# Attention in units of 256 tokens and four heads, with queries and keys from split float32r products

## The chip, the cores and the metric

The kernel runs on one core of a Trainium2 chip. The core has five engines with an instruction queue each: TensorE (PE, matmuls into PSUM), VectorE (DVE), ScalarE (ACT), GpSimd (POOL) and SyncE (SP, which here issues transfers). They run side by side and wait for each other by semaphores only. The metric is the device time of one launch in microseconds, lower is better.

## The reference

A model of four parts runs over 2,048 tokens of 128 channels: windowed attention, an FFN, a delta-rule layer with an MLP, and a routed FFN, with a layer norm behind each. Only the first part matters here:

```python
H, D, window_size = (16, 64, 32)
xn = x * rsqrt(mean(x * x) + 1e-6)
q, k, v = split(xn @ w_qkv.T, 3)              # each 2048 x 1024, 16 heads of 64
q = apply_rope(q, cos, sin)                   # (x1*c - x2*s, x2*c + x1*s) in each head
k = apply_rope(k, cos, sin)
attn = einsum('bhqd,bhkd->bhqk', q, k) / sqrt(64)
mask = (q_pos >= k_pos) & (q_pos - k_pos <= window_size)
out = softmax(where(mask, attn, -1e9)) @ v
x = layernorm(x + out @ w_out.T)
```

## The kernel before, in words

The program is written out by hand: each engine has its own list of instructions in a fixed order, and loops over `u` in range(32) interleave units at different depths of the pipeline. A *unit* is one block of 128 tokens and 8 of the 16 heads (`G` = 2 units a block). In iteration u the engines do the following.

- PE: scores of unit u (L551), output projection of u-4 (L596), queries (`project_qk(u+3, 0)`, L523) and keys of u+3, with the transpose of the attention output of u-3 (L583) between them, the product with V of u-2 (`attend`, L574), V of u+2 (`project_v`, L537 to L539), the transpose of the probabilities of u-1 (L560). Queries and keys are plain f32 matmuls, which run as two passes each; V is made of three float32r products of a high and a low part (`xv_high`, `xv_low`, `wv_high`, `wv_low`).
- DVE: adds the masks and takes maxima (`mask_scores(u)`, L974), adds the residual of u-4 (L1002), multiplies queries and keys of u+3 by the cosine and by the sine out of PSUM (`rope_products`, L965, four instructions of 512 columns), normalises the output of u-2 (L983, L985). In some iterations it also scales a block of x (`normalise_x`, L1052), makes the low part of the transposed x (`split_x`, L993 and L994) and layer norm statistics.
- SP: `swap_halves(u+3)`, four transfers (L448) that copy `t_sin` to `t_swap` with the halves of each head exchanged. In even iterations `move_v` goes ahead of it, six transfers (L456 to L462) that bring V of a block, shifted by 32 tokens, to `v_before`. Loads of x, of the rope tables and of late weights stand between them.
- POOL: `rope_sum(u)`, two instructions (L1601) that add `t_cos` and `t_swap` into `qk`, and the copy of the last 32 keys (L1594). Its first work is the inverse root mean square of x (`inverse_rms`, L1614 and L1617), for the second group of x in iteration 2.
- ACT: exponentials (L1358) and copies out of PSUM.

`t_cos`, `t_sin` and `t_swap` have two buffers, by u modulo 2. So DVE's products of unit u wait for the rope sum of unit u-2:

```python
dve.wait_ge(qk_ps, 2 * u + j + 1)
wait(dve, rope_done, 2 * (u - 1))
```

The program as it was before, where the change touches it:

Of the kernel before, what the change touches and what calls it, by code (L numbers as in the profile page):

```python
# [11 lines left out]
ALU = mybir.AluOpType  # L12
# [50 lines left out]
def build(nc, x, w_q, w_k, w_v, w_o, late_weights, row_vectors, kv_bias, out, late):  # L63
# [22 lines left out]
    V_SLOTS = 3  # L86
# [4 lines left out]
    XT_STEP = {2 * n - 5: n for n in range(GB, NB)}  # L91
# [51 lines left out]
    with ExitStack() as ctx:  # L143
# [43 lines left out]
        xnT = sb("xnT", [P, T])  # L187


        wv_high = sb("wv_high", [P, INNER], F32R)  # L190
        wv_low = sb("wv_low", [P, INNER], F32R)
        xv_high = sb("xv_high", [P, NB, P + D], F32R)
        xv_low = sb("xv_low", [P, NB, P + D], F32R)
# [3 lines left out]
        t_cos = sb("t_cos", [P, G, GH, P])  # L197
        t_sin = sb("t_sin", [P, G, GH, P])
        t_swap = sb("t_swap", [P, G, GH, P])
        qk = sb("qk", [P, G, GH, WINDOW + P])  # L200
        zeros = sb("zeros", [P, PAIRS, WINDOW])
# [4 lines left out]
        v_own = sb("v_own", [P, V_SLOTS, 2, H // 2, DV])  # L206
        v_before = sb("v_before", [P, 2, 2, H // 2, DV])
# [94 lines left out]
        swapped = [sem(f"swapped{g}") for g in range(G)]  # L302
        stored = sem("stored")
# [32 lines left out]
        wq_scaled = sem("wq_scaled")  # L336
# [98 lines left out]
        def _(sp):  # L435
# [6 lines left out]
            def swap_halves(u, sides=(0, 2)):  # L442

                sp.wait_ge(rope_products_done, 2 * u + sides[1])
                c = slice(PAIRS * sides[0], PAIRS * sides[1])
# [4 lines left out]
            def move_v(b):  # L450

                sp.wait_ge(qk_zeroed, 3)
                sp.wait_ge(v_kept, G * b + G)
                wait(sp, o_ps, G * b - G)
                to, own, last = v_before[:, b % 2], v_own[:, b % V_SLOTS], v_own[:, (b - 1) % V_SLOTS]
                sp.dma_start(to[32:64], own[0:32]).then_inc(v_moved[b % 2], 16)  # L456
                sp.dma_start(to[96:128], own[64:96]).then_inc(v_moved[b % 2], 16)
                sp.dma_start(to[64:96, 0], own[32:64, 0]).then_inc(v_moved[b % 2], 16)
                sp.dma_start(to[0:32, 1], own[96:128, 1]).then_inc(v_moved[b % 2], 16)
                if b > 0:  # L460
                    sp.dma_start(to[64:96, 1], last[32:64, 1]).then_inc(v_moved[b % 2], 16)
                    sp.dma_start(to[0:32, 0], last[96:128, 0]).then_inc(v_moved[b % 2], 16)  # L462
# [7 lines left out]
            load_rope(0, slice(0, P))  # L470
# [9 lines left out]
            for u in range(UNITS):  # L480
                if u % G == 0:
                    move_v(u // G)
                if u + 3 < UNITS:
                    swap_halves(u + 3)
                for q in range(1, TG):
                    if u == UG * q - 7:
                        load_rope(2, slice(512 * q, 512 * q + 512))
                    if q > 1 and u == UG * q - 16:
                        load_x(q)
# [1281 lines left out]
```

## Time and profile before

| | |
|---|---|
| Three timed runs | 467.13, 476.39, 472.85 us; median 472.85 |
| Profiled execution | 466.78 us, of it 465.0 us span |
| Busy share of the span | PE 87%, DVE 70%, ACT 55%, POOL 36% |
| Chain that ended last, by engine | PE 52%, DVE 16%, SP's queue 11%, ACT 7%, issue 5%, DMA 5%, POOL 4% |
| Same chain, largest lines | QK L523 7%, SP L448 6%, VY L596 4%, DMA t_swap 4% |

The span is what the profile covers of the execution. Busy shares are means over stages that differ: the attention takes about the first 225 us. Issuing a transfer isn't counted as busy, so SP has no share of its own; it shows up as SPq in the chain. A wait names what ended it.

### The profile page before, as it was taken

The numbers are of one execution on the slowest core, as the hardware profiler recorded it, in microseconds if no ns is written. First come the engines' busy times: TensorE is split into PE (matmuls) and PEld (weight loads), VectorE is DVE, ScalarE is ACT, GpSimd is POOL, SyncE is SP. The second block draws the span as 40 slices with busy tenths as digits, with TensorE's granted clock in tenths as the row PEclk, the third lists the DMA queues.
The fourth block names the chain that finished last, engine by engine and source line by source line (L and its number), as shares of the span: only waits on it lengthen the run. The fifth ranks groups of instructions, "written<-read, shape, count | busy, mean of one in ns | idle before, by whom it ended". The sixth has DMA issues, their size and how long they took to land.

```text
span 465.0 us, 18396 instructions
## 1 busy us (share of the span) xinstructions
PE 406.5 (87%) x7464; PEld 357.1 (77%) x7464; DVE 324.6 (70%) x1583; ACT 254.4 (55%) x669; POOL 168.2 (36%) x192
## 2 busy tenths in 40 slices
PE   1888999989999899998999897999994989889780
PEld 1777899989889789997866776998994677767670
DVE  1577779878889599878454677863027896888564
ACT  3245665656655465666554584224401467986937
POOL 2465556443365544454064540040007673000012
PEclk9999999999999999999999998999998899999986
DMA  7466655774555656655000000000000000000003
GB/s 237 106 146 189 142 137 129 188 174 114 143 129 154 168 133 143 178 160 140 9 2 0 2 1 3 3 4 1 1 1 0 2 1 2 1 1 1 2 0 90
DMA packets 20515, 35.34 MB, mean 76 GB/s; under 512 B 4368, under 2 KB 11536, under 8 KB 20432
## 3 DMA queue, kind: packets, MB, share of 16 engines
q1 hardware_dynamic: 19856, 33.12, 28.3%
q8 instruction: 59, 0.97, 0.9%
q10 hardware_dynamic: 576, 1.05, 0.8%
q14 instruction: 24, 0.20, 0.1%
HBM read 7.81 MB, written 1.05 MB: 19 GB/s over the span
## 4 chain that ended last, share of the span: by engine, by line
PE 52%; DVE 16%; SPq 11%; ACT 7%; issue 5%; DMA 5%; POOL 4%; DVEq 0%; ACTq 0%; POOLq 0%
PE QK L523 7%; SPq L448 6%; PE VY L596 4%; DMA t_swap<-t_sin 4%; PE O L680 3%; PE O L574 3%; PE S L551 3%; POOL qk L1601 2%; PE QK L747 2%; PE O L751 2%; DVE unread_tests L1267 2%; DVE t_sin L965 2%; PE PT L560 2%; PE PT L583 2%; PE S L778 2%
## 5 line engine op out<-in xcount | busy, mean ns | idle before, releaser
L1601 POOL TENSOR_TENSOR qk<-t_cos,t_swap 128x512 f32<-128x512 f32 x64 | 80.5, 1280 | 104.1 <-DMA t_swap<-t_sin 100.5
L1358 ACT ACTIVATE probs<-probs,negative_max 128x64 f32<-128x64 f32 x256 | 67.9, 339 | 44.0 <-DVE negative_max L974 44.0
L965 DVE TENSOR_TENSOR t_cos<-QK,cos 128x512 f32<-128x512 f32 x64 | 44.0, 688 | 32.6 <-POOL qk L1601 21.3
L1633 POOL TENSOR_TENSOR rstd<-var_eps,minus_half 128x4 f32<-128x4 f32 x24 | 25.4, 1058 | 101.2 <-DVE var_eps L1037 81.4
L965 DVE TENSOR_TENSOR t_sin<-QK,sin 128x512 f32<-128x512 f32 x64 | 43.5, 680 | 0.0
L974 DVE CUSTOM_DVE_ANT_0 probs<-S,masks 128x64 f32<-128x64 f32 x256 | 39.2, 217 | 6.1 <-PE S L551 5.8
L523 PE MATMUL QK<-xnT,wq 128*128 128x128 f32 x256 | 36.3, 287 | 2.6 <-DVE t_sin L965 1.9
L1373 ACT COPY v_own<-VY 128x512 f32<-128x512 f32 x32 | 18.8, 587 | 35.9 <-PE VY L539 35.9
L596 PE MATMUL VY<-wo,oT 128*128 128x128 f32 x256 | 36.8, 287 | 0.7 <-ACT oT L1379 0.7
L523 PEld LDWEIGHTS QK<-xnT,wq 128*128 128x128 f32 x256 | 32.8, 201 | 3.9 <-DVE t_sin L965 2.3
L523 PE MATMUL QK<-xnT,wk 128*128 128x128 f32 x256 | 35.5, 283 | 0.1
L596 PEld LDWEIGHTS VY<-wo,oT 128*128 128x128 f32 x256 | 31.1, 191 | 3.9 <-ACT oT L1379 0.9
L523 PEld LDWEIGHTS QK<-xnT,wk 128*128 128x128 f32 x256 | 32.6, 199 | 0.9 <-DVE t_sin L965 0.9
L551 PE MATMUL S<-qk 64*32 64x64 f32 x2048 | 28.3, 224 | 3.9 <-POOL qk L1601 3.4
L551 PEld LDWEIGHTS S<-qk 64*32 64x32 f32 x2048 | 22.8, 105 | 9.9 <-POOL qk L1601 5.0
L574 PE MATMUL O<-v_own,probsT 64*32 64x65 f32 x1024 | 27.5, 225 | 1.3 <-issue 1.3
L574 PE MATMUL O<-v_before,probsT 64*32 64x65 f32 x1024 | 26.8, 224 | 0.0
L1379 ACT COPY oT<-PT 128x512 f32<-128x512 f32 x32 | 18.5, 578 | 13.0 <-PE PT L583 12.7
L574 PEld LDWEIGHTS O<-v_before,probsT 64*32 64x32 f32 x1024 | 21.4, 105 | 4.1 <-issue 0.8
L985 DVE TENSOR_TENSOR o_sb<-O,inv_total 128x512 f32<-128x512 f32 x32 | 22.1, 691 | 1.1
L537 PE MATMUL VY<-wv_high,xv_high 128*128 128x256 f32 x64 | 21.1, 330 | 1.1 <-issue 0.8
L574 PEld LDWEIGHTS O<-v_own,probsT 64*32 64x32 f32 x1024 | 20.5, 105 | 1.5 <-issue 1.5
(284 smaller groups left out, 1053.5 us busy)
## 6 DMA issues: line engine op xcount, KB each, us to landing
t_swap<-t_sin SPq DMA_DIRECT2D x124, 128.0 KB
v_before<-v_own SPq DMA_DIRECT2D x32, 132.0 KB
v_before<-v_own SPq DMA_DIRECT2D x62, 66.0 KB
late_tile<-late_weights SPq DMA_DIRECT2D x7, 189.0 KB, 3.7
x_sb<-x SPq DMA_DIRECT2D x4, 256.0 KB, 4.5
out<-XA SPq DMA_DIRECT2D x4, 256.0 KB, 2.3
cos<-rope_cos SPq DMA_DIRECT2D x3, 256.0 KB, 3.5
sin<-rope_sin SPq DMA_DIRECT2D x3, 256.0 KB, 5.6
```

Source lines behind the costliest of these rows:

```text
L448: sp.dma_start(t_swap[other:other + D // 2, u % G, c], t_sin[r:r + D // 2, u % G, c]).then_inc(swapped[u % G], 16)
L523: last = nc.tensor.matmul(QK[j][:, m * P:(m + 1) * P], w[:, f], xnT[:, block_of(u)], start=True, stop=True)
L537: nc.tensor.matmul(to, xv_high[:, b, tok], wv_high[:, f], start=True, stop=False)
L551: last = nc.tensor.matmul(S[WINDOW * i:WINDOW * i + WINDOW, e ^ (i // 2), m, :], qk[r, half(u), m, WINDOW * (i + 1):WINDOW * (i + 2)], qk[ ...
L574: last = nc.tensor.matmul(O_ps[WINDOW * i:WINDOW * i + WINDOW, e, m, 0:D + 1], probsT[r, half(u), m, WINDOW * i:WINDOW * i + WINDOW], v[:, ...
L596: last = nc.tensor.matmul(VY[:, 0:C], oT[:, n, :], wo[:, n, :], start=(m == 0), stop=(m == PAIRS - 1))
L965: last = nc.vector.tensor_tensor(dst[:, u % G, PAIRS * j:PAIRS * j + PAIRS], QK[j][:].rearrange("p (m t) -> p m t", m=PAIRS), table[:, tok ...
L974: last = nc.vector.tensor_tensor_reduce(out=probs[:, u % G, m, e, :], in0=S[:, e, m, :], in1=masks[:, min(u // G, 1), :], scale=-1.0, scal ...
L985: nc.vector.tensor_tensor(o_sb[:, u % G].rearrange("p m e d -> p e m d"), O_ps[:, :, :, 0:D], totals.broadcast_to([P, 2, PAIRS, D]), ALU.m ...
L1358: last = nc.scalar.activation(probs[:, u % G, m, e, :], probs[:, u % G, m, e, :], ACT.Exp, scale=-1.0, bias=negative_max[:, u % G, e, m:m ...
L1601: nc.gpsimd.tensor_tensor(qk[:, h, c, WINDOW:WINDOW + P], t_cos[:, h, c], t_swap[:, h, c], ALU.add).then_inc(rope_done, 1)
L1633: nc.gpsimd.tensor_tensor(rstd[:, grp(q)], var_eps[:, grp(q)], minus_half[:, grp(q)], ALU.pow).then_inc(roots_done, 1)
```

## The change

A unit is now two blocks, 256 tokens, and four heads: `HG` = 4 units to a pair of blocks, and still 32 units. Buffers by u modulo 2 stay; `qk` gets four. Queries and keys are now made as V is: weights are split into a high and a low float32r part, and each result of 256 columns is the sum of three products. `xv_high` and `xv_low` hold each block twice, end to end, and serve both. Splitting the weights is new work at the start, on ACT, DVE and POOL. `normalise_x` moves from DVE to ACT, `split_x` becomes one instruction of 256 columns, the residual works on 256 columns. `move_v` serves a window of two units: six transfers in the first two windows, eight from then on, for the same bytes. At the start PE runs 56 small bfloat16 matmuls; x is transposed and split by halves; the keys' swap of unit 0 is issued by ACT; x is loaded and scaled one iteration or more earlier, and the second group's `inverse_rms` stands ahead of the first rope sum.

```diff
+    BT = 2 * P
+    HG = 4
+    MP = H // HG // 2
+    V_SLOTS = 4
-    XT_STEP = {2 * n - 5: n for n in range(GB, NB)}
+    XT_STEP = {2 * n - 7: n for n in range(GB, NB)}
...
-            def move_v(b):
+            def move_v(w):
                 sp.wait_ge(qk_zeroed, 3)
-                sp.wait_ge(v_kept, G * b + G)
-                wait(sp, o_ps, G * b - G)
+                sp.wait_ge(v_kept, 2 * w + 2)
+                wait(sp, o_ps, 2 * w - 2)
...
+                sp.dma_start(to[32:64], own[0:32]).then_inc(v_moved[w % 2], 16)
+                sp.dma_start(to[96:128], own[64:96]).then_inc(v_moved[w % 2], 16)
+                sp.dma_start(to[64:96, :, 0], own[32:64, :, 0]).then_inc(v_moved[w % 2], 16)
+                sp.dma_start(to[0:32, :, 1], own[96:128, :, 1]).then_inc(v_moved[w % 2], 16)
+                sp.dma_start(to[64:96, 1, 1], own[32:64, 0, 1]).then_inc(v_moved[w % 2], 16)
+                sp.dma_start(to[0:32, 1, 0], own[96:128, 0, 0]).then_inc(v_moved[w % 2], 16)
+                if w >= 2:
+                    sp.dma_start(to[64:96, 0, 1], last[32:64, 1, 1]).then_inc(v_moved[w % 2], 16)
+                    sp.dma_start(to[0:32, 0, 0], last[96:128, 1, 0]).then_inc(v_moved[w % 2], 16)
...
             def project_qk(u, j):
-                for m in range(PAIRS):
-                    f = slice((PAIRS * half(u) + m) * P, (PAIRS * half(u) + m + 1) * P)
-                    last = nc.tensor.matmul(QK[j][:, m * P:(m + 1) * P], w[:, f], xnT[:, block_of(u)], start=True, stop=True)
+                for m in range(MP):
+                    f = slice((MP * g + m) * P, (MP * g + m + 1) * P)
+                    to = QK[j][:, m * BT:(m + 1) * BT]
...
+                    nc.tensor.matmul(to, high[:, f], xv_high[:, xs, 0], start=True, stop=False)
+                    nc.tensor.matmul(to, low[:, f], xv_high[:, xs, 0], start=False, stop=False)
...
+                    last = nc.tensor.matmul(to, high[:, f], xv_low[:, xs, 0], start=False, stop=True)
                 last.then_inc(qk_ps, 1)
...
+            pe.wait_ge(warm_set, 1)
+            for _ in range(56):
+                nc.tensor.matmul(QK[0][:, 0:P], warm_bf[:], warm_bf[:], start=True, stop=True)
...
+            def split_x(n):
+                dve.wait_ge(xv_staged, n - 1)
+                nc.vector.tensor_tensor(xv_low[:, n % XV], xnT[:, n % GB].unsqueeze(1).broadcast_to([P, 2, P]),
+                                        xv_high[:, n % XV].bitcast(F32), ALU.subtract).then_inc(xv_split, 1)
...
+            def normalise_x(n):
+                act.wait_ge(rms_done, n // GB + 1)
+                nc.scalar.mul(xn[:, n, :], x_sb[:, n, :], rms[:, n:n + 1]).then_inc(x_scaled, 1)
...
+            act.wait_ge(rope_products_done, 2)
+            for r in range(0, P, D // 2):
+                other = r ^ (D // 2)
+                act.dma_start(t_swap[other:other + D // 2, 0, MP:], t_sin[r:r + D // 2, 0, MP:]).then_inc(first_keys_swapped, 16)
...
                 for q in range(1, TG):
-                    if u == UG * q - 6:
+                    if u == UG * q - 8:
                         inverse_rms(q + 1, GB * q, GB * q + GB)
                 rope_sum(u)
```

On SP, in a period of two units in the middle of the attention, the order was this, where a row of eight is the swap of an odd unit and then that of the next even one:

```order
L448 DMA t_swap<-t_sin 32x1024 x8
L493 DMA late_tile<-late_weights 128x378
L456 DMA v_before<-v_own 32x1056
L457 DMA v_before<-v_own 32x1056
L458 DMA v_before<-v_own 32x528
L459 DMA v_before<-v_own 32x528
L461 DMA v_before<-v_own 32x528
L462 DMA v_before<-v_own 32x528
L448 DMA t_swap<-t_sin 32x1024 x8
```

and it becomes this:

```order
L462 DMA t_swap<-t_sin 32x1024 x8
L510 DMA late_tile<-late_weights 128x378
L471 DMA v_before<-v_own 32x1056
L472 DMA v_before<-v_own 32x1056
L473 DMA v_before<-v_own 32x2x264
L474 DMA v_before<-v_own 32x2x264
L475 DMA v_before<-v_own 32x264
L476 DMA v_before<-v_own 32x264
L478 DMA v_before<-v_own 32x264
L479 DMA v_before<-v_own 32x264
L462 DMA t_swap<-t_sin 32x1024 x8
```

Two transfers more stand between the swaps, and four of the eight are half as large as the smallest before.

On ACT, from its first work to the first exponentials, the order was:

```order
L1398 ACTIVATE wq<-wq 128x512 x2
L1400 COPY xnT<-PT 128x512
L1385 CAST xv_high<-xnT 128x4x128
L1386 CAST xv_high<-xnT 128x4x64
L1405 CAST wv_high<-wv 128x512 x2
L1411 ACTIVATE xn,stat<-x_sb 128x128 x4
L1373 COPY v_own<-VY 128x2x4x64 x2
L1358 ACTIVATE probs<-probs,negative_max 128x64 x8
```

and it becomes:

```order
L1460 ACTIVATE wq_high<-wq 128x512
L1461 CAST wk_high<-wk 128x512
L1448 CAST xv_high<-PT 128x2x128 x2
L1460 ACTIVATE wq_high<-wq 128x512
L1461 CAST wk_high<-wk 128x512
L1448 CAST xv_high<-VY 128x2x128 x2
L1473 CAST wv_high<-wv 128x512 x2
L1479 DMA t_swap<-t_sin 32x512 x4
L1483 ACTIVATE xn,stat<-x_sb 128x128 x4
L1426 COPY v_own<-VY 128x8x64 x2
L1411 ACTIVATE probs<-probs,negative_max 128x64 x8
```

The squares of the second group of x (`stat`) now come behind the four transfers of unit 0's keys, which wait for DVE's first products.

## Rows read from the trace of the kernel before

**Rows 1.** Windows: busy us of PE, PEld, DVE, ACT, POOL; granted clock, DMA share.

```profile
60.00:100.00 40.00, 38.58 (x1053) 35.38 (x1053) 33.18 (x154) 24.39 (x81) 19.23 (x21) 1.00 0.65 156
100.00:140.00 40.00, 38.87 (x1032) 35.46 (x1021) 34.41 (x154) 24.92 (x84) 20.07 (x22) 1.00 0.55 133
```

**Rows 2.** Waits, 35 to 215 us: total in us, times, longest.

```profile
POOL qk L1601 <- DMA t_swap<-t_sin: 87.8, 23, 9.3
ACT probs L1358 <- DVE negative_max L974: 34.7, 28, 3.9
DVE t_cos L965 <- POOL qk L1601: 15.2, 7, 4.5
```

**Rows 3.** SP's waits from 60 to 200 us: total, times, longest.

```profile
SPq L448 <- DVE t_sin L965: 11.7, 8, 2.9
```

**Rows 4.** Timeline of SP, 111 to 128 us: start, duration, instruction, count.

```profile
111.52 3.39 SPq L448 DMA_DIRECT2D t_swap<-t_sin  x4
...
115.65 0.51 SPq L456 DMA_DIRECT2D v_before<-v_own  x1
...
117.47 2.07 SPq L459 DMA_DIRECT2D v_before<-v_own  x1
...
120.85 6.64 SPq L448 DMA_DIRECT2D t_swap<-t_sin  x8
```

**Rows 5.** Timeline of POOL at 127 us; in brackets idle time and releaser.

```profile
126.86 2.50 POOL L1601 TENSOR_TENSOR qk<-t_cos,t_swap 128x512 f32<-128x512 f32 x2 [6.97 <-DMA t_swap<-t_sin]
```

**Rows 6.** Timeline of DVE, 129 to 139 us.

```profile
129.47 0.69 DVE L965 TENSOR_TENSOR t_cos<-QK,cos 128x512 f32<-128x512 f32 x1 [1.55 <-POOL qk L1601]
...
132.71 1.22 DVE L1052 TENSOR_SCALAR xn<-x_sb,rms 128x128 f32<-128x128 f32 x1
...
135.46 0.68 DVE L965 TENSOR_TENSOR t_cos<-QK,cos 128x512 f32<-128x512 f32 x1
...
137.52 0.68 DVE L965 TENSOR_TENSOR t_sin<-QK,sin 128x512 f32<-128x512 f32 x1
```

**Rows 7.** Timeline of DVE where the products of units 9 and 31 begin.

```profile
64.28 0.69 DVE L965 TENSOR_TENSOR t_cos<-QK,cos 128x512 f32<-128x512 f32 x1 [2.06 <-POOL qk L1601]
208.50 0.69 DVE L965 TENSOR_TENSOR t_cos<-QK,cos 128x512 f32<-128x512 f32 x1 [1.41 <-POOL qk L1601]
```

**Rows 8.** Chain that ended last, 99 to 106 us: start, duration, piece.

```profile
101.42 0.89 PE QK L523 x8
...
104.75 0.12 PE VY L538
```

**Rows 9.** Groups on DVE, 35 to 215 us; then one line's min/median/max.

```profile
L1052 DVE TENSOR_SCALAR xn<-x_sb,rms 128x128 f32<-128x128 f32 x12 | 7.7, 640 | 0.0
L994 DVE TENSOR_TENSOR xv_low<-xnT,xv_high 128x64 fp32r<-128x64 f32 x12 | 5.8, 486 | 0.0
L993 DVE TENSOR_TENSOR xv_low<-xnT,xv_high 128x128 fp32r<-128x128 f32 x12 | 5.2, 435 | 0.0
L1002 DVE TENSOR_TENSOR r<-r,VY 128x128 f32<-128x128 f32 x13 | 3.6, 279 | 0.0
L1052 DVE TENSOR_SCALAR xn<-x_sb,rms x12: 275/584/1318, 42.1 to 185.9; 128x128 f32<-128x128 f32 x12
```

**Rows 10.** Timeline of all engines, 0 to 31 us.

```profile
10.46 2.08 PE L523 MATMUL QK<-xnT,wq 128*128 128x128 f32 x8 [0.68 <-ACT xnT L1400]
...
12.31 0.30 ACT L1411 ACTIVATE xn<-x_sb 128x128 f32<-128x128 f32 x1
...
20.61 2.50 POOL L1601 TENSOR_TENSOR qk<-t_cos,t_swap 128x512 f32<-128x512 f32 x2 [5.62 <-DMA t_swap<-t_sin]
...
28.77 1.02 POOL L1617 TENSOR_TENSOR rms<-mean,minus_half 128x4 f32<-128x4 f32 x1
```

**Rows 11.** Timeline of SP, 13 to 36 us.

```profile
31.91 2.50 SPq L448 DMA_DIRECT2D t_swap<-t_sin  x4
34.45 0.59 SPq L439 DMA_DIRECT2D x_sb<-x  x1
```

More of the change, by code:

```diff
@@ L196, in build @@
         rms = sb("rms", [P, NB])
[L197 to L201, printed above, removed]
+        t_cos = sb("t_cos", [P, G, 2 * MP, BT])
+        t_sin = sb("t_sin", [P, G, 2 * MP, BT])
+        t_swap = sb("t_swap", [P, G, 2 * MP, BT])
+        qk = sb("qk", [P, HG, 2 * MP, WINDOW + BT])
+        zeros = sb("zeros", [P, MP, WINDOW])
         negative_max = sb("negative_max", [P, G, 2, PAIRS])
@@ L533, in project_v @@
+                last.then_inc(qk_ps, 1)
+            def project_v(v):
+                b, h = 2 * (v // 4) + v % 2, v % 4 // 2
+                pe.wait_ge(xv_split, max(2, b - 1))
+                wait(pe, r1_done, v - 5)
+                wait(pe, v_kept, v)
+                wait(pe, xT_kept, sum(s <= v - 2 for s in XT_STEP))
                 for e in range(2):
-                    tok = slice(D * e, D * e + P)
-                    f = slice((half(u) * 2 + e) * GH * D // 2, (half(u) * 2 + e + 1) * GH * D // 2)
+                    high, low = (t[:, b % XV].rearrange("p d t -> p (d t)")[:, D * e:D * e + P] for t in (xv_high, xv_low))
+                    f = slice((h * 2 + e) * GH * D // 2, (h * 2 + e + 1) * GH * D // 2)
@@ L540, in project_v @@
+                    last = nc.tensor.matmul(to, low, wv_high[:, f], start=False, stop=True)
                 last.then_inc(v_ps, 1)
@@ L563, in attend @@
             def attend(u):
-                b = u // G
+                w = u // 2
                 pe.wait_ge(probsT_done, u + 1)
-                pe.wait_ge(v_moved[b % 2], 96 * (b // 2 + 1) - 32 * (1 - b % 2))
+                pe.wait_ge(v_moved[w % 2], 96 + 128 * (w // 2))
                 wait(pe, o_kept, u)
-                for m in range(PAIRS):
+                for s in range(PAIRS):
+                    b, m = s // MP, s % MP
                     for i in range(P // WINDOW):
@@ L593, in project_out @@
                 wait(pe, r1_done, u)
-                for m in range(PAIRS):
-                    n = PAIRS * half(u) + m
-                    last = nc.tensor.matmul(VY[:, 0:C], oT[:, n, :], wo[:, n, :], start=(m == 0), stop=(m == PAIRS - 1))
+                for s in range(PAIRS):
+                    b, m = s // MP, s % MP
+                    last = nc.tensor.matmul(VY[:, P * b:P * b + P], oT[:, PAIRS * half(u) + s, :], wo[:, MP * (u % HG) + m, :],
+                                            start=(m == 0), stop=(m == MP - 1))
                 last.then_inc(y_ps, 1)
             def transpose_x(n, u):
-                pe.wait_ge(x_normalised, n + 1)
+                pe.wait_ge(x_scaled, n - GB + 1)
                 pe.wait_ge(v_kept, u + 2)
@@ L1395, in _ @@
                 act.dma_start(half(wk, h), half(w_k, h)).then_inc(ld_qk[h], 16)
[L1396 to L1401 removed]
+            split_qk_weights(0)
+            stage_first_x(0)
+            split_qk_weights(1)
+            stage_first_x(1)
             act.wait_ge(ld_wv, 16)
@@ L1619, in _ @@
             inverse_rms(1, 0, GB)
+            for h in range(G):
+                w = slice(h * GH * D, (h + 1) * GH * D)
+                pool.wait_ge(qk_weights_high, 2 * h + 2)
+                nc.gpsimd.tensor_tensor(wk_low[:, w], wk[:, w], wk_high[:, w].bitcast(F32), ALU.subtract).then_inc(wk_low_done, 1)
             pool.wait_ge(wv_split, 1)
```

242 lines of the change are left out of this document (132 added, 110 removed).

## The prediction

> **What bounds the kernel now.** I read the busy times by stretch first, since the change lies almost wholly in the attention stage, from about 10 to 225 us of the span. There TensorE (PE) is busy for 38.6 and 38.9 us in two stretches of 40 us [rows 1]. That looks like the bound, and the change relieves it. But a modelled PE at 97% doesn't say who sets the pace, so I read the waits of this stage next [rows 2]. GpSimd (POOL) waits 87.8 us for the transfers t_swap<-t_sin, and VectorE (DVE) waits 15.2 us, in 7 stretches, for GpSimd's rope sum. Behind PE's busy time runs a ring: products of sine and cosine (DVE, L965), four transfers that swap the halves (issued by SP, L448), the sum (POOL, L1601), and then the products two units later, which need the same buffers.
>
> Third, SP's own queue. Over the 140 us from 60 to 200 it waits for DVE's products for only 11.7 us in all [rows 3]: it issues for 92% of the time. One issue takes 0.59 us and 0.04 to the next, and some are long (2.07 us) [rows 4]. So the scarce thing between two swaps is SP's time to issue.
>
> Now I go once round the ring, two periods of two units each [rows 4 to 6]. The swap of unit 16 starts at 111.52, right behind its products. Behind it SP issues a late load and the six transfers of V, and only at 120.85 the swap of unit 17, whose products were long done: 9.3 us. The sum starts at 126.86, 6.0 us after the first of its four issues, and takes 2.5 (to 129.36). The products of unit 19 start at 129.47, at once. Those of unit 20 start at 135.46: DVE worked without a gap in between (6.0 us). They end at 138.20, where the next swap starts: 2.7 us. The sum is 9.3 + 6.0 + 2.6 + 6.0 + 2.7 = 26.6 us for two periods, 13.3 for one. The mean of eleven periods, from the products of unit 9 to those of unit 31, is (208.50 - 64.28) / 11 = 13.1 us [rows 7]. PE's own demand is 38.9/40 of that, 12.7, so both bounds lie close together, the ring a little ahead.
>
> **The change, part by part.**
>
> *QK products.* Eight matmul passes of 128 columns for a bank take 0.89 us, and the change puts six f32r passes of 256 columns there. The V products show such a pass at 0.12 us [rows 8]. So 0.72 instead of 0.89, twice a unit: 0.34 us of PE a unit, 0.7 a period. On the ring only one half lies open (the second half of an even unit's products, inside the 2.7 us): -0.17 a round.
>
> *V transfers.* With v_before holding two blocks by four heads, move_v issues eight transfers instead of six, from the third window on, for the same bytes. They stand between the swap of an even unit and that of the odd one, inside the 9.3 us. Two issues at 0.63 are 1.27 us. Long ones come on top: 92% of 13.1 us is 12.1 of issuing a period, of which 14 transfers and about 1.3 loads (21 in 16 periods) at 0.63 are 9.6; the other 2.5 are 0.16 an issue. So +0.3 for the two new ones. For issues and runs of 1,056 bytes the trace has no row; I take the 0.59 that transfers of both present sizes take, as lower bound nothing (if they fell where SP waits anyway) and as upper bound 2.07 each.
>
> *DVE.* normalise_x (L1052) goes to ScalarE: 12 instructions of 0.64 us mean, one a period, 1.22 in the round shown [rows 6, 9]. It lies in the 6.0 us. Splitting x becomes one instruction for two (0.44 + 0.49 mean); its 256 columns I bound by 0.4 us and the 1.3 that L1052 takes at its longest, and take 0.7: -0.2, but behind an even unit's products, off this path. The residual grows from 128 to 256 columns, 0.28 to an assumed 0.41 us (half of an instruction on 128 columns is start-up, since the products take 0.69 for 512): +0.13. In the 6.0 us: -0.5. Bounds there: nothing, if GpSimd's work slows the rest of DVE as it seems to slow this instruction (0.28 us at its shortest, 1.32 at its longest), and -1.1 as in the round shown.
>
> *The rest of a period* costs nothing I can find: ScalarE takes 0.3 us of normalise_x a period, is 61% busy, and its cover is that its waits for DVE's maxima sum to 34.7 us [rows 1, 2]; if those vanished, its later exponentials would delay PE's transposes by those 0.3. Key tails on GpSimd halve, in the shadow of its waits for the swap. Four qk buffers take away a wait of GpSimd for scores, which has room in those same waits.
>
> So a round costs +1.27 +0.3 -0.5 -0.17 = +0.9 us, a period +0.45. Windows 2 to 14 have the longer transfers ahead of an odd swap: 13 x 0.45 = +5.9 us. A second sum agrees: SP would issue 17.3 x (0.63 + 0.16) = 13.7 us a period, with nothing to spare. PE's demand falls to 12.0.
>
> *The start.* Products of unit 0 begin sooner: PE's warm matmuls may bring the first eight QK passes from 2.08 us to the 0.9 of later ones [rows 8, 10], and the keys' swap no longer stands behind the queries' on SP. I expect them from about 11 us to 13.7. But ScalarE now issues four transfers, some 2.4 us, before it squares the second group of x (4 x 0.3 us), and GpSimd makes inverse_rms of that group (0.19 + 1.02 us) ahead of the first rope sum, not at unit 2 as before. What is queued behind is everything: 13.7 + 2.4 + 1.2 + 1.5 = 18.9 us for the first sum instead of 20.61 [rows 10]. That is 1.7 earlier. Then SP has a load of x and two more V issues ahead of unit 3's swap, +1.9: that swap starts at 31.9 + 0.2 [rows 11], as now. Unit 4's swap, which today waits behind that load, comes 0.7 earlier. Start: -0.8, between +0.5 and -2.
>
> *The tail.* The last two tiles finish together, one more bn_stats and bn_aggr (0.4 us) on DVE, hidden by PE's own work of the FFN; the later stages are untouched.
>
> Sum: 466.8 (this execution, span 465.0) + 5.9 - 0.8 = 471.9 us. This execution lies 6.1 us under the median of the three runs shown, and these with it average 470.8, 4 above it. I add 3 for that: **475 us**.
>
> Here a rule speaks the other way. The profile shows issues as 92% of SP's time. The Trainium skill (DMA: Bandwidth & Descriptors, Issuing engines are not separate DMA queues) says that the time to initiate a DMA "is usually small relative to the DMA itself". The rows disagree with it here; by it the two added issues would be free, and the sum would be that of the first rival.
>
> **The rivals.**
>
> *Issues are hidden anyway.* If the two new ones fell where SP waits, a round would be -0.5 -0.17, a period -0.35, 13 of them -4.5, with the start -5.3: 461.5 + 3 = 464.5. For it: SP waits 11.7 us somewhere. Against: it waits before even units' swaps, and the issues stand before the odd ones'. Chance 0.20.
>
> *PE was the bound.* If each period had been PE's 12.7, it would now be 12.0: 14 x -0.7 = -10, and the start gains 3.5 us, if GpSimd isn't held: its first two instructions would then end at some 19.6 instead of 23.1: 453 + 3 = 456. For it: 97% busy. Against: the seven stretches in which DVE waited for the rope sum. Chance 0.08.
>
> *SP falls behind for good* (the other side). Its place is SP's queue between swaps; it decides from the point where SP no longer waits for DVE at all, 11.7 us in 140, 1.1 a period, which the added 1.3 use up. Then each long issue shifts everything. In rows 4 the eleven issues from 111.52 to 120.80 are long by 0.87 us in the first swap and 1.48 in L459, 0.21 each instead of 0.16. At that a period of 17.3 issues is 17.3 x 0.84 = 14.5 us, +1.4, and 13 of them +18; with the start and the 3 us that is 487. For it: transfers of 1,056-byte runs double the pieces of four of eight V transfers. Against: a late SP finds its earlier transfers landed, which should make issues short. Chance 0.20.
>
> *The change doesn't do what it says* for PE would be f32r passes of 256 columns at more than 0.12 us for these operands; that costs PE only its spare time.
>
> **The numbers.** The forecast itself has 0.50, a slow f32r pass the last 0.02. Its own range is 470 to 480: 13 periods of between +0.1 and +0.8. To hold 8 in 10 I go from 463 (below the first rival) to 486 (just short of the third). About 2%, 9.5 us, is what a measurement of this kernel can tell from no change. Faster by over 2%, below 463.4: the PE rival and a little of the first, 0.10. Slower, above 482.3: nearly all of the third rival and the forecast's upper tail, 0.22. Within 2%: 0.68.
>
> **What would show it.** Steps right: SP without a wait in the attention stage; POOL still waiting some 90 us for t_swap; about 13.5 us from one odd unit's products to the next; PE's busy share down to some 90%, with QK at 0.72 us for six passes; the first rope sum at about 19 us, behind inverse_rms. Wrong: periods under 12.8 with SP waiting for DVE; DVE's products waiting for QK and not for the sum; or new waits of PE for v_moved.

## The result, and the profile after

| | before | after |
|---|---|---|
| median of 20 runs, us | 472.47 (463.34 to 483.16) | 478.94 (475.92 to 494.24) |
| profiled execution, us (span) | 466.78 (465.0) | 479.43 (477.6) |
| mean granted TensorE clock | 0.977 | 0.956 |

The changed kernel is slower: its time is 1.028 times that of before (95% interval 1.024 to 1.032). The comparisons here and below leave out disturbed runs, so they can differ from a quotient of medians, and the traces of five variants (the two V transfers on ScalarE, the shared swap in either kernel, unit 3's swap on ScalarE, no warm matmuls) come from such runs and are read below for issues, waits and periods up to the end of the attention stage, not for the time.

First the same windows of the attention stage as in [rows 1], and a stretch at its end that comes up below:

```profile
60.00:100.00 40.00, 36.47 (x954) 32.41 (x950) 31.26 (x145) 24.23 (x78) 18.44 (x20) 1.00 0.61 144
100.00:140.00 40.00, 35.69 (x962) 31.43 (x962) 30.04 (x132) 22.59 (x72) 18.55 (x20) 1.00 0.57 136
225.00:235.00 10.00, 6.12 (x154) 5.36 (x152) 4.87 (x39) 4.03 (x14) 2.48 (x2) 0.78 0.41 92
```

In the first two windows PE was busy for 38.6 and 38.9 of 40 us; now it is for 36.5 and 35.7. It got less to do, and the program still takes longer. In the chain that ended last, over the whole span, SP's queue went from 11% to 25% and PE from 52% to 31%. The waits of the stage (total, times, longest) answer [rows 2]:

```profile
POOL qk L1678 <- DMA t_swap<-t_sin: 100.5, 22, 7.9
ACT probs L1411 <- DVE negative_max L1009: 44.4, 27, 3.6
DVE t_cos L1000 <- POOL qk L1678: 30.3, 15, 3.8
...
PE VY L635 <- DVE r L1051: 7.8, 10, 1.7
...
PE QK L549 <- DVE xv_low L1026: 2.5, 3, 1.4
```

GpSimd waits 100.5 us for the swapped halves instead of 87.8, and VectorE 30.3 us, in 15 stretches instead of 7, for GpSimd's rope sum. PE's own new waits are small: 7.8 us for the residual and 2.5 for the low part of x. Then SP's wait from 60 to 200 us, for [rows 3]:

```profile
SPq L462 <- DVE t_sin L1000: 2.1, 4, 0.9
```

In 140 us SP waits for 2.1 us instead of 11.7: it issues practically all the time. Its timeline shows one period (start, duration, instruction), as in [rows 4]:

```profile
99.57 6.39 SPq L462 DMA_DIRECT2D t_swap<-t_sin  x8
106.00 1.95 SPq L510 DMA_DIRECT2D late_tile<-late_weights  x1
108.05 0.51 SPq L471 DMA_DIRECT2D v_before<-v_own  x1
108.60 0.59 SPq L472 DMA_DIRECT2D v_before<-v_own  x1
...
111.83 0.59 SPq L478 DMA_DIRECT2D v_before<-v_own  x1
112.46 0.59 SPq L479 DMA_DIRECT2D v_before<-v_own  x1
113.10 7.57 SPq L462 DMA_DIRECT2D t_swap<-t_sin  x8
...
121.40 0.51 SPq L471 DMA_DIRECT2D v_before<-v_own  x1
```

From one V transfer's start to the next window's (108.05 to 121.40) SP has no gap above 0.11 us between these rows. The eight V issues fill 5.0 us, and the eight swap issues that follow take 7.57, 0.95 each, so there are long ones among them. The products of units 9 and 31 [rows 7] begin on VectorE at:

```profile
66.72 0.69 DVE L1000 TENSOR_TENSOR t_cos<-QK,cos 128x512 f32<-128x512 f32 x1 [1.86 <-POOL qk L1678]
...
217.21 0.69 DVE L1000 TENSOR_TENSOR t_cos<-QK,cos 128x512 f32<-128x512 f32 x1 [3.40 <-POOL qk L1678]
```

(217.21 - 66.72) / 11 = 13.68 us for a period, where 13.11 was.

Where did the 12.65 us between the two profiled executions arise? I follow the rope sum of three units through both traces. That of unit 3 starts at 39.06 instead of 36.25: +2.8 us at the start. That of unit 31 starts at 228.78 instead of 218.08, 10.7 later: +7.9 in the steady part, 14 periods. What comes behind adds 2.0 more. There the window from 225 to 235 us shows a granted clock of 0.78, with PE busy for 6.1 of 10 us while it waits for the last swap. Before, the same window had 1.00. An output projection, eight matmuls of one shape, in the chains that ended last (not of the same unit):

```profile
229.55 0.89 PE VY L596 x8
```

```profile
228.78 2.49 POOL qk L1678 x2
...
232.50 2.00 PE VY L626 x8
```

0.89 us before and 2.00 after, right behind the wait: at half the clock (1.2 GHz for 2.4). The shift between the two kernels, 10.7 us at unit 31's rope sum, is 13.0 at the next stage's first matmuls of L680, now L715 (240.42 and 253.43 us), and changes little from there on: the 2.0 us arise in this stretch.

### The profile page after: what moved, and what is told of

Its sections match the earlier page's. It is cut to its first block, busy times and chain, and to the rows that moved or that the text cites. A ratio compares the mean times of both kernels' runs of the same rounds, so it can differ in the third digit from the quotient of the medians.

```text
span 477.6 us, 18293 instructions
## 1 busy us (share of the span) xinstructions
PE 407.9 (85%) x7392; PEld 354.4 (74%) x7392; DVE 322.4 (68%) x1563; ACT 257.9 (54%) x672; POOL 168.5 (35%) x193
## 3 DMA queue, kind: packets, MB, share of 16 engines
HBM read 7.81 MB, written 1.05 MB: 19 GB/s over the span
## 4 chain that ended last, share of the span: by engine, by line
PE 31%; SPq 25%; DVE 20%; issue 7%; ACT 6%; DMA 6%; POOL 4%; ACTq 1%; DVEq 0%; POOLq 0%
SPq L462 12%; DMA t_swap<-t_sin 5%; PE O L715 3%; DVE t_sin L1000 3%; POOL qk L1678 3%; PE QK L782 2%; PE O L786 2%; SPq L475 2%; DVE unread_tests L1320 2%; SPq L474 2%; DVE t_cos L1000 2%; PE S L813 2%; PE QK L923 1%; SPq L471 1%; PE QK L679 1%
## 5 line engine op out<-in xcount | busy, mean ns | idle before, releaser
L1000 DVE TENSOR_TENSOR t_cos<-QK,cos 128x512 f32<-128x512 f32 x64 | 43.9, 685 | 39.4 <-POOL qk L1678 37.3
L580 PE MATMUL S<-qk 64*32 64x64 f32 x2048 | 29.3, 227 | 9.3 <-POOL qk L1678 7.3
L626 PEld LDWEIGHTS VY<-wo,oT 128*128 128x128 f32 x256 | 32.1, 196 | 4.1 <-ACT oT L1432 1.0
L1426 ACT COPY v_own<-VY 128x512 f32<-128x512 f32 x32 | 18.8, 586 | 28.2 <-PE VY L566 28.1
L604 PE MATMUL O<-v_own,probsT 64*32 64x65 f32 x1024 | 28.7, 233 | 0.1
L545 PE MATMUL QK<-xv_high,wq_high 128*128 128x256 f32 x64 | 21.5, 335 | 3.8 <-DVE t_sin L1000 3.4
L613 PE MATMUL PT<-ident,o_sb 128*128 128x128 f32 x128 | 19.9, 279 | 2.7 <-DVE o_sb L1020 2.5
L604 PEld LDWEIGHTS O<-v_own,probsT 64*32 64x32 f32 x1024 | 21.6, 109 | 0.3 <-issue 0.3
L545 PE MATMUL QK<-xv_high,wk_high 128*128 128x256 f32 x64 | 21.4, 334 | 0.3 <-DVE t_sin L1000 0.2
L549 PE MATMUL QK<-xv_low,wq_high 128*128 128x256 f32 x64 | 19.3, 302 | 2.6 <-DVE xv_low L1026 2.5
```

The source lines that it names most:

```text
L545: nc.tensor.matmul(to, high[:, f], xv_high[:, xs, 0], start=True, stop=False)
L580: last = nc.tensor.matmul(S[WINDOW * i:WINDOW * i + WINDOW, e ^ (i // 2), s, :], qk[r, u % HG, m, WINDOW + at:2 * WINDOW + at], qk[r, u % ...
L604: last = nc.tensor.matmul(O_ps[WINDOW * i:WINDOW * i + WINDOW, e, s, 0:D + 1], probsT[r, half(u), s, WINDOW * i:WINDOW * i + WINDOW], v[:, ...
L626: last = nc.tensor.matmul(VY[:, P * b:P * b + P], oT[:, PAIRS * half(u) + s, :], wo[:, MP * (u % HG) + m, :], start=(m == 0), stop=(m == M ...
L1000: last = nc.vector.tensor_tensor(dst[:, u % G, MP * j:MP * j + MP], QK[j][:].rearrange("p (m t) -> p m t", m=MP), table[:, tok].unsqueeze( ...
```

## The experiments

Two theories stood against each other. **A:** SP's queue of issues paces the attention; the two added V transfers, 0.6 to 0.8 us each, are the cost. **B:** the issues are hidden, and the cost comes from TensorE's passes, VectorE's work, smaller pieces or the start. All ratios are to the kernel before, with 95% intervals; the change as a whole has 1.028 (1.024 to 1.032).

### The added issues alone, on the kernel before

```diff
-                sp.dma_start(to[64:96, 0], own[32:64, 0]).then_inc(v_moved[b % 2], 16)
-                sp.dma_start(to[0:32, 1], own[96:128, 1]).then_inc(v_moved[b % 2], 16)
+                for c in (slice(0, PAIRS), slice(PAIRS, 2 * PAIRS)):
+                    sp.dma_start(to[64:96, 0, c], own[32:64, 0, c]).then_inc(v_moved[b % 2], 16)
+                    sp.dma_start(to[0:32, 1, c], own[96:128, 1, c]).then_inc(v_moved[b % 2], 16)
...
```

The two waits for `v_moved` count to 128 instead of 96 accordingly.

> The kernel before, with its two largest V transfers of a window cut in two along the pairs: eight issues on SP instead of six, the same bytes, nothing else changed. Theory A (SP's queue of issues is the scarce part of the ring): 1.3 us of issues and up to 0.3 of long ones stand in front of every odd unit's swap, half of it in each of the two periods of a round is not right - it is once a period of two units, so a round of the ring that spans both swaps grows by 0.6 to 1.6 us, and over some 13 windows the time grows by 6 to 14 us; SP's waits between 60 and 200 us fall from 11.7 us to under 5. Theory B (issues are hidden, and what slowed the changed kernel is on DVE, at the start and at the end): within 2 us of the kernel before. Theory C (the size of the pieces, under 2 KB, makes the landing slow): this run has smaller pieces too, so it should show the swap of the halves landing later than 5.4 us after its first issue on the mean; by A that stays as it is.

Measured: 1.044 (1.034 to 1.055). SP's wait and the products of units 9 and 31:

```profile
SPq L448 <- DVE t_sin L966: 5.5, 6, 1.7
```

```profile
67.59 0.68 DVE L966 TENSOR_TENSOR t_cos<-QK,cos 128x512 f32<-128x512 f32 x1
...
216.05 0.69 DVE L966 TENSOR_TENSOR t_cos<-QK,cos 128x512 f32<-128x512 f32 x1 [1.74 <-POOL qk L1602]
```

The period is 13.50 us. From an even unit's swap to the odd one's it takes 10.03 us in the mean of 13 rounds, where before has 8.89 and the changed kernel 10.02: the two issues alone make the whole of this step. From an odd unit's first issue to its sum it takes 5.62 us (before 5.40, after 5.54), so smaller pieces matter little. In time the kernel lost more than I expected (6 to 14 us), but how much is uncertain: the profiled execution is 11.95 us above that of before, the second run that counts 4.6 above that one, and the mean of these two (481.0 us) is 3.2% above that of before in the same round of measurements (466.0), where the ratio on record says 4.4%. With nothing but the issues added, B falls. That this kernel is slower than the changed one isn't shown: its profiled execution is 0.7 us below that one's, and its period is shorter (13.50 for 13.68).

### The added issues taken off SP, in the changed kernel

```diff
-                if w >= 2:
-                    sp.dma_start(to[64:96, 0, 1], last[32:64, 1, 1]).then_inc(v_moved[w % 2], 16)
-                    sp.dma_start(to[0:32, 0, 0], last[96:128, 1, 0]).then_inc(v_moved[w % 2], 16)
...
+            def move_v_across(w):
+                act.wait_ge(o_ps, 2 * w - 2)
+                to, last = v_before[:, w % 2], v_own[:, (w - 2) % V_SLOTS]
+                act.dma_start(to[64:96, 0, 1], last[32:64, 1, 1]).then_inc(v_moved[w % 2], 16)
+                act.dma_start(to[0:32, 0, 0], last[96:128, 1, 0]).then_inc(v_moved[w % 2], 16)
...
+                if u % 2 == 0 and 4 <= u < UNITS:
+                    move_v_across(u // 2)
```

> The changed kernel, with the two transfers that bring V across a window issued by ScalarE at the end of even units, not by SP. SP is back to six V issues a window. Theory A (SP's queue): the odd swap starts 1.3 to 1.6 us earlier in each window, the period falls from 13.68 to about 13.1 us, and the time by 6 to 10 us, to about 470; SP's waits between 60 and 200 us rise from 2.1 us towards 10. Theory B (something else on the ring): under 2 us. If ScalarE's own issues delay its exponentials, PE waits for it and the gain is smaller: each issue costs ScalarE some 0.6 us, 1.2 a window.

Measured: 0.998 (0.993 to 1.002), 3% below the changed kernel. The same two transfers move the same bytes; only the queue that issues them is another.

```profile
SPq L462 <- DVE t_sin L997: 9.6, 9, 2.3
```

```profile
65.89 0.69 DVE L997 TENSOR_TENSOR t_cos<-QK,cos 128x512 f32<-128x512 f32 x1 [0.80 <-POOL qk L1683]
...
207.72 0.69 DVE L997 TENSOR_TENSOR t_cos<-QK,cos 128x512 f32<-128x512 f32 x1 [3.54 <-POOL qk L1683]
```

SP waits 9.6 us again, the period is 12.89, and even swap to odd swap takes 8.79. The gain of about 14 us is above the 6 to 10 expected.

### TensorE's passes as before, in the changed kernel

```diff
-                    nc.tensor.matmul(to, high[:, f], xv_high[:, xs, 0], start=True, stop=False)
-                    nc.tensor.matmul(to, low[:, f], xv_high[:, xs, 0], start=False, stop=False)
...
-                    last = nc.tensor.matmul(to, high[:, f], xv_low[:, xs, 0], start=False, stop=True)
+                    for i in range(2):
+                        last = nc.tensor.matmul(to[:, P * i:P * i + P], high[:, f].bitcast(F32),
+                                                xv_high[:, xs.start + i, 0].bitcast(F32), start=True, stop=True)
```

> The changed kernel, with Q and K computed by plain f32 matmuls of 128 columns on the high parts alone (the products with the low parts of x and of the weights are left out), eight passes a bank as in the kernel before. It puts TensorE's QK cost back to 0.89 us for 0.72. Theory A (the ring of products, swap and sum sets the period): the time changes by less than 3 us, and the open half of an even unit's products grows by 0.17 us in one round at most. Theory C (TensorE sets the period): 0.34 us a unit more, over 32 units some 10 us slower.

Measured: 1.036 (1.030 to 1.042), 0.8% or some 4 us above the changed kernel, with intervals that just overlap. Eight passes take 0.89 us again, as in [rows 8], in a chain (60 to 130 us) whose largest part is SP's swap issues, 18.6%:

```profile
88.32 0.89 PE QK L548 x8
```

```profile
68.26 0.69 DVE L1000 TENSOR_TENSOR t_cos<-QK,cos 128x512 f32<-128x512 f32 x1 [1.86 <-POOL qk L1678]
...
219.46 0.69 DVE L1000 TENSOR_TENSOR t_cos<-QK,cos 128x512 f32<-128x512 f32 x1 [3.37 <-POOL qk L1678]
```

The period is 13.74 us: +0.06, where TensorE as the bound would give +0.68. Unit 3's sum starts 1.8 us later. So PE doesn't set the pace, though its passes cost something at the start; A's bound of 3 us was a little low.

### Half of each swap issued by ScalarE, in both kernels

In the changed kernel, and with the names of before in that one:

```diff
...
-                for r in range(0, P, D // 2):
+                for r in rows:
...
-                    swap_halves(u + 3)
+                    swap_halves(u + 3, rows=(0, D // 2))
...
+                if u + 3 < UNITS:
+                    act.wait_ge(rope_products_done, 2 * (u + 3) + 2)
+                    for r in (D, D + D // 2):
+                        other = r ^ (D // 2)
+                        act.dma_start(t_swap[other:other + D // 2, (u + 3) % G], t_sin[r:r + D // 2, (u + 3) % G]).then_inc(swapped[(u + 3) % G], 16)
```

> The changed kernel, with two of the four transfers that swap a unit's halves issued by ScalarE for units from 3 on, behind its wait for the products; SP issues the other two. It takes four of 16 issues a period, 2.5 us, off SP's queue, and a swap's first to last issue goes from four in a row to two. Theory A: SP waits again for 15 us or more between 60 and 200 us, the odd swap starts 1.3 us earlier (two issues of the even swap are gone) and each sum follows its products 1.2 us earlier; the period falls from 13.68 to 12.7 or less, where TensorE's own work of 12.0 or ScalarE bounds it: 460 to 466 us. Theory B (SP's issues are hidden): no gain, and a loss from the 2.5 us that ScalarE's issues take in a period of its 13.7.

> The kernel before, with two of the four transfers of each swap from unit 3 on issued by ScalarE. The ring loses 1.3 us between an even unit's swap and the odd one's, and 1.3 between a swap's first issue and its sum. If the ring were alone, the period would fall from 13.1 to under 12.5; but here TensorE's work is 12.7 us a period (QK at 0.89 for eight passes), so by my account TensorE becomes the bound: period 12.7 to 12.8, 4 to 6 us faster. The changed kernel with the same edit had 12.0 to 12.5 us in most periods and gained 4.3% against itself unedited. By the rival (PE's demand is not a floor but overlaps), this kernel would gain as much, 4%.

Measured: the changed kernel with it 0.986 (0.979 to 0.992), the kernel before with it 1.003 (0.997 to 1.009). The windows and SP's waits, first of the changed kernel so edited:

```profile
100.00:140.00 40.00, 39.44 (x1005) 35.82 (x999) 36.19 (x168) 26.98 (x86) 21.42 (x25) 1.00 0.58 154
```

```profile
SPq L462 <- DVE t_sin L1000: 27.1, 11, 4.4
```

and of the kernel before so edited, with VectorE's wait for PE's queries and keys:

```profile
100.00:140.00 40.00, 39.90 (x1053) 36.77 (x1055) 35.70 (x166) 26.77 (x89) 20.15 (x22) 1.00 0.54 149
```

```profile
SPq L448 <- DVE t_sin L965: 43.3, 12, 5.1
```

```profile
DVE t_cos L965 <- PE QK L523: 5.7, 17, 0.5
```

The same relief of SP is worth over 4% after the change and nothing before it. Before, PE is then busy for 39.9 of 40 us, and VectorE waits 17 times for its queries and keys: most periods are 12.5 to 12.8 us, PE's 12.7 as forecast. Changed, eight of eleven are 11.8 to 12.7, close to PE's 12.0. With SP relieved in both, the changed kernel takes 1.8% less than the one before, where without it it takes 2.8% more. That fits a saving on PE that SP's queue had hidden, but it doesn't show how much of the 1.8% is PE's: over all eleven periods the means of these two traces are 12.99 us changed (two are about 16) and 12.83 before, and no run puts PE's old passes into the changed kernel with the shared swap. The time of the kernel before I had expected to fall by 4 to 6 us, and that failed. In its trace the products of unit 31 do begin at 203.58 us, 4.9 sooner than in [rows 7], while that execution as a whole is 3.4 us longer than the one of before. As it is not one of those that count, its later stages don't tell where the counted ones lose the gain. That stays open.

### The splitting of x on GpSimd

```diff
-                if u - 1 in XT_STEP:
-                    split_x(XT_STEP[u - 1])
...
+                if u - 3 in XT_STEP:
+                    n = XT_STEP[u - 3]
+                    pool.wait_ge(xv_staged, n - 1)
+                    nc.gpsimd.tensor_tensor(xv_low[:, n % XV], xnT[:, n % GB].unsqueeze(1).broadcast_to([P, 2, P]),
+                                            xv_high[:, n % XV].bitcast(F32), ALU.subtract).then_inc(xv_split, 1)
```

> The changed kernel, with the splitting of x (the one subtraction of 256 columns, 0.85 us mean on VectorE, once a period) moved from VectorE to GpSimd, ahead of the rope sum of an even unit, where GpSimd waits for the swap. Theory A with its second part (the splitting stands in the stretch of VectorE between an odd unit's products and the next even unit's, which is part of the ring): that stretch falls from 5.71 to about 4.9 us and the period by up to 0.42 us, the time by 3 to 6 us, if nothing else fills the gap, such as a wait for transposes of the probabilities. Rival (that stretch is paced by TensorE's work anyway): under 1.5 us, with a new wait of VectorE for a PE result inside it. If GpSimd needs over 1.3 us for it, its rope sum of the even unit may start late, and the gain is lost.

Measured: 1.032 (1.023 to 1.040): no gain. The group on GpSimd, from 60 to 200 us, and SP's wait:

```profile
L1725 POOL TENSOR_TENSOR xv_low<-xnT,xv_high 128x256 fp32r<-128x256 f32 x10 | 7.4, 738 | 0.0
```

```profile
SPq L462 <- DVE t_sin L1000: 2.0, 5, 0.6
```

VectorE's stretch from odd to even products fell from 5.71 to 5.07 us (means of 14), as theory A's second part had it, but the period stayed at 13.60: SP came to the even swap 1.05 us behind the products instead of 0.56. Neither reading was right. With SP's queue full, 0.64 us less on VectorE ahead of it only made SP later behind the products.

### The start

ScalarE's squares ahead of the keys' transfers:

```diff
-            act.wait_ge(rope_products_done, 2)
-            for r in range(0, P, D // 2):
-                other = r ^ (D // 2)
-                act.dma_start(t_swap[other:other + D // 2, 0, MP:], t_sin[r:r + D // 2, 0, MP:]).then_inc(first_keys_swapped, 16)
...
                 squares(n)
+            act.wait_ge(rope_products_done, 2)
+            for r in range(0, P, D // 2):
+                other = r ^ (D // 2)
+                act.dma_start(t_swap[other:other + D // 2, 0, MP:], t_sin[r:r + D // 2, 0, MP:]).then_inc(first_keys_swapped, 16)
```

> The changed kernel, with ScalarE squaring the second group of x (4 x 0.3 us) before it issues the four transfers of the keys' swap of unit 0, as my account of the start has it: the first rope sum waits for inverse_rms, and that for ScalarE's squares, which stand behind 2.4 us of issues. If that chain sets the start, the first sum comes at 18 to 19 us instead of 20.95 and the time falls by up to 2.4 us. Rival (unit 3's swap, behind two more V issues and the load on SP, sets when the steady pace begins, and it depends on SP alone): the first sum comes earlier, unit 3's sum stays at 39 us, and the time changes by less than 1 us.

Measured: 1.022 (1.014 to 1.030), some 3 us below the changed kernel, within what the intervals allow for none. GpSimd's timeline:

```profile
18.38 2.53 POOL L1678 TENSOR_TENSOR qk<-t_cos,t_swap 128x512 f32<-128x512 f32 x2 [0.82 <-DMA t_swap<-t_sin]
...
37.38 2.48 POOL L1678 TENSOR_TENSOR qk<-t_cos,t_swap 128x512 f32<-128x512 f32 x2 [6.10 <-DMA t_swap<-t_sin]
```

The first sum comes 2.6 us sooner, at 18.38, and that of unit 3 still 1.7 sooner. The chain through ScalarE's issues did hold the first sum.

Unit 3's swap on ScalarE:

```diff
-                if u + 3 < UNITS:
+                if 0 < u < UNITS - 3:
                     swap_halves(u + 3)
...
+                if u == 0:
+                    act.wait_ge(rope_products_done, 8)
+                    for r in range(0, P, D // 2):
+                        other = r ^ (D // 2)
+                        act.dma_start(t_swap[other:other + D // 2, 1], t_sin[r:r + D // 2, 1]).then_inc(swapped[1], 16)
```

> The changed kernel, with the swap of unit 3 alone, all four transfers, issued by ScalarE right behind the products (29.6 us), and not by SP, where it is issued at 33.85, behind a load of x and the six V transfers of the first window. This asks what the start costs. If the late swap of unit 3 shifts the rest one for one: its sum comes at some 36 us for 39.06, the sum of unit 5 too, and the time falls by 2.5 to 4 us. Rival (SP's queue is the ring from then on, so that only the number of its issues counts; four of 125 swap issues less are 2.5 us): the gain is 2.5 us as well but appears as SP's lead, and unit 5's sum moves by less than 1.5 us at once. If ScalarE is late for it because it waits for VectorE's maxima, nothing is gained.

Measured: 1.024 (1.013 to 1.034), not told apart from the changed kernel. On GpSimd the sums of units 3 and 5:

```profile
36.68 2.52 POOL L1683 TENSOR_TENSOR qk<-t_cos,t_swap 128x512 f32<-128x512 f32 x2 [3.33 <-DMA t_swap<-t_sin]
...
50.99 1.28 POOL L1683 TENSOR_TENSOR qk<-t_cos,t_swap 128x512 f32<-128x512 f32 x1 [6.81 <-DMA t_swap<-t_sin]
```

Unit 3's sum came 2.4 us sooner (36.68 for 39.06), but unit 5's started at 50.99, where the changed kernel has 49.87. The lead was gone two units later: SP, relieved of unit 3, had to wait for the products of unit 4, which end at 35.97, and came to unit 5's swap at 44.12, where the changed kernel has 44.57; then the landing took 6.9 us for 5.3.

And without the 56 warm matmuls (the loop over `range(56)` taken out):

> The changed kernel without its 56 warming matmuls at the start. In the changed kernel PE is idle for 3.4 us behind them and the first QK passes run at half pace (0.21 us) up to some 15.5 us all the same. If the warming does nothing: the same time within 1 us. Rival (it brings the clock up sooner than it would come): the first products start later than 13.2 us, and the time rises by 1 to 4 us.

Measured: 1.032 (1.022 to 1.043), no difference in time that shows. Unit 0's products start at 13.05 us without and 13.23 with them. The trace does show one: without them PE's passes stay 0.21 us apart until 21.5 us, with them only until 15.5. The first rope sum comes at 20.78 us without and 20.95 with them all the same, since it waits for the chain through ScalarE.

### The best version

The shared swap and the squares first, together, and then the splitting of x on GpSimd as well:

> The changed kernel with two edits that each helped alone: two of the four transfers of each swap from unit 3 on issued by ScalarE, and ScalarE's squares of the second group of x ahead of the keys' transfers at the start. If the two add up: the first rope sum at about 18.4 us for 20.95, units 3 and 4 some 1.5 to 2.5 us earlier, the period as with the shared swap (12.0 to 12.5 us in most, where TensorE's 12.0 is the floor). That gives 98.55% of the kernel before, less 2 us or 0.4%: a ratio of 0.98. If the start does not reach the end: 0.985 as with the shared swap alone.

> The same as the kernel with the shared swap and the squares first, and the splitting of x on GpSimd too, not on VectorE. With SP's queue full that edit alone gave nothing: VectorE's stretch fell from 5.71 to 5.07 us, and SP's lateness behind even products rose from 0.56 to 1.05. With SP relieved, VectorE's stretch could count. Theory A (TensorE's 12.0 us of work a period is now the floor): the same within 2 us. Rival (the ring through VectorE still sets the pace): 0.6 us of VectorE less in a round, up to 0.3 to 0.6 us a period, 4 to 8 us faster.

Measured: 0.981 (0.974 to 0.989) and 0.981 (0.970 to 0.991). The first beats both kernels: 1.9% under the kernel before, with an interval wholly below 1, and 4.5% under the changed one. Its span, its windows and SP's wait:

```profile
core 0: 454.7 us, clock 0.972
```

```profile
100.00:140.00 40.00, 39.32 (x1080) 35.28 (x1064) 37.05 (x158) 26.41 (x82) 22.46 (x24) 1.00 0.58 151
```

```profile
SPq L462 <- DVE t_sin L1000: 26.4, 11, 3.2
```

PE is back at 39 of 40 us, now with shorter periods (12.59 us in the mean of the eleven). VectorE's 0.6 us were worth nothing that shows here either, as expected where PE is the floor.

## Why the prediction came out as it did

The forecast was 475 us in a range of 463 to 486, with no change beyond 2% as the likeliest. Measured: 478.94, and slower by 2.8%, the side that had 0.22. The direction of the bound was right, the size was not: between two such executions I had forecast +5.1 us (466.8 to 471.9), and it was +12.65. That the time still came near the forecast is partly luck, as the paragraph behind the steps shows. By its steps:

- **The bound, right.** The ring through SP was the limit, not PE at 97%. The two runs that touch only the number of SP's issues moved the time by +3.2 to +4.4% and -3%; the one that touches only PE's passes moved it by under 1%. In the kernel before the two bounds lay close together, as the forecast had it: with half of each swap off SP its period fell only from 13.11 to 12.83 us, and its time didn't fall.
- **The V transfers, right, a little less than the term.** Forecast +1.57 us from even to odd swap, measured +1.13 (8.89 to 10.02). Counted in the timeline, SP issues 164 times from 60 to 200 us before and 176 times after, so (140 - 11.7) / 164 = 0.782 and (140 - 2.1) / 176 = 0.784 us each. So 1.13 is about two short issues of 0.63 less a little; the 0.3 for long ones fell elsewhere in the period, since the mean price of an issue stayed.
- **VectorE's -0.5 us a round, wrong.** Odd to even products took 5.65 before and 5.71 after in the mean of 14 rounds (5.74 and 5.58 without the first of them): at most -0.2, not -0.5. I had put the splitting of x behind an even unit's products, "off this path". The timeline has it behind an odd unit's (`XT_STEP` names odd steps and the splitting comes one later), just where `normalise_x` had been, with a mean of 0.85 us for the 0.7 forecast:

```profile
121.08 0.69 DVE L1000 TENSOR_TENSOR t_cos<-QK,cos 128x512 f32<-128x512 f32 x1 [1.22 <-POOL qk L1678]
...
124.32 1.29 DVE L1026 TENSOR_TENSOR xv_low<-xnT,xv_high 128x256 fp32r<-128x256 f32 x1
...
126.76 0.41 DVE L1051 TENSOR_TENSOR r<-r,VY 128x256 f32<-128x256 f32 x1
127.10 0.68 DVE L1000 TENSOR_TENSOR t_cos<-QK,cos 128x512 f32<-128x512 f32 x1
```

  Here it takes 1.29 us of the 6.0 between the two products. The residual is right (0.41 for 0.41). But as the splitting on GpSimd showed, this error cost nothing of its own: with SP full, the -0.5 would not have come off the period anyway. What failed is that I added terms around one ring when another resource without slack took its place.
- **A period, +0.57 us for +0.45.** My "second sum" was the better one: 17.3 issues at 0.78 are 13.5 us, against 13.68 measured and 13.55 from the ring. It said "nothing to spare", and that is the condition I gave for the rival in which SP falls behind for good: SP no longer waits for VectorE. It did come about; its price didn't. I had let each issue grow to 0.84 us, and they stayed at 0.78.
- **QK, right.** Passes start 0.12 us apart, as in V's [rows 8]:

```profile
70.15 0.28 PE L546 MATMUL QK<-xv_high,wq_low 128*128 128x256 f32 x1
70.27 0.28 PE L549 MATMUL QK<-xv_low,wq_high 128*128 128x256 f32 x1
```

- **The start, wrong: -0.8 forecast, +2.8 measured.** Three parts failed. Unit 0's products began at 13.23 and not at about 11: the warm matmuls ended 3.4 us before x's transposes, and the first passes came 0.21 us apart, at 1.2 GHz (granted clock 0.50 from 10 to 15 us), for 0.12 later:

```profile
12.49 0.41 PE L546 MATMUL QK<-xv_high,wq_low 128*128 128x256 f32 x1
12.70 0.41 PE L549 MATMUL QK<-xv_low,wq_high 128*128 128x256 f32 x1
```

  The first sum waits for the chain I had named, at 20.95 instead of 18.9 (the terms I gave for it add to 18.8):

```profile
15.76 2.52 ACTq L1479 DMA_DIRECT2D t_swap<-t_sin  x4
...
18.32 0.31 ACT L1483 ACTIVATE xn<-x_sb 128x128 f32<-128x128 f32 x1 [4.65 <-DVE t_sin L1000]
...
19.69 0.19 POOL L1692 TENSOR_SCALAR mean<-stat 128x4 f32<-128x4 f32 x1 [3.42 <-ACT xn L1483]
...
19.97 1.01 POOL L1695 TENSOR_TENSOR rms<-mean,minus_half 128x4 f32<-128x4 f32 x1
...
20.95 1.27 POOL L1678 TENSOR_TENSOR qk<-t_cos,t_swap 128x512 f32<-128x512 f32 x1
```

  Four issues of ScalarE, the squares, the mean, the inverse and then the sum follow each other as forecast, only 2 us later. And unit 3's swap, forecast at 32.1, was issued at 33.85, 1.9 later than before; its sum followed 5.2 us behind that, where it had been 4.3. These two make up the +2.8.
- **The tail, +2.0 for 0.** I had taken the later stages as untouched. They are, but between unit 31's rope sum and the next stage the shift grew by 2.3 us, where the granted clock was low behind PE's wait for the last swap (2.00 us for 0.89). Before, PE waited there for the rope sum too, 1.3 us instead of 3.7, and kept 1.00. That the longer wait is what lowered the clock is likely, not shown by a run of its own.

The start (3.6 us), the steady part (2.0) and the tail (2.0) make up what separates 471.9 from the 479.4 of the profiled execution. That the median came only 4 us above the forecast is because I had added 3 us for a quick profiled execution of before, while that of after lies at its own median. That part of the agreement is luck: the 3 us stood for nothing in the change, and they hide a good third of the 7.5 us that the terms missed.

On the rule cited beside the forecast: two issues moved from SP to ScalarE with the same bytes gave 3%. The Trainium skill (DMA: Bandwidth & Descriptors, Issuing engines are not separate DMA queues) says that this saves only the sequencer's time to initiate, "usually small relative to the DMA itself". That moving the issues saves time on the queue of SP agrees with these runs. That it is small doesn't hold here, where 5.5 us pass from a swap's first issue to its sum, 2.5 of them for its four issues, and one queue initiates 16 to 18 transfers in 13.7 us.

## What to carry to other kernels

Count the issues of each queue in a period, multiply by the mean price that the trace gives (here 0.78 us) and hold the product against the period before you add a transfer: at 92% two small ones are no longer free. A queue that is full makes savings elsewhere worthless, and can hide real ones; spread its issues first and measure the other change after. When a change moves work, look up in the timeline which unit's stretch it lands in, and don't trust the step's name.

## What the hardware showed that I had not expected

- The mean price of an issue on SP is nearly the same in all kernels (0.75 to 0.78 us from 60 to 200 us, for 127 to 179 issues), with transfers from 33 to 189 KB. A short issue takes 0.5 to 0.6 us at any of these sizes, and single ones take up to 2.7 us (in the changed kernel with the shared swap). What makes an issue long stays open.
- ScalarE issues at no higher price while it does its own work: in the best version its 44 issues from 60 to 200 us take 0.65 us in the mean, those of SP 0.71 (without the time between two). That version has 58 issues more on ScalarE, and is faster.
- PE's clock behind a wait: in the stretch in which PE waited for the last swap (busy 6.1 of 10 us) it was granted 0.78, and the output projection behind it took 2.00 us for 0.89. While it was busy for over 35 of 40 us, between 60 and 140 us, it was granted 1.00 in both kernels. But from 140 to 180 us, with PE busy for 37.3 of 40, the changed kernel was granted 0.96.
